# A TensorE-bound mixture-of-experts kernel: all SBUF buffers laid out in another order and at rounder addresses

## What is computed

```python
x = x + 0.5 * ffn(layernorm(x)); x = x + attn(layernorm(x)); x = x + 0.5 * ffn(layernorm(x))

def ffn(x):                                   # E = 64 experts, D = 128, F = 64, TOP_K = 8
    shared = silu(x @ Ws_up) @ Ws_down
    aff = x @ centroids.T
    idx = top_k(aff + expert_biases, 8)
    w = sigmoid(aff[idx]);  w = w / sum(w)    # cw: w at the 8 chosen experts, 0 at the others
    h = silu(einsum('td,edf->etf', x, W_up))
    y = einsum('etf,efd->etd', h, W_down)
    return shared + einsum('etd,te->td', y, cw)

def attn(u):
    xf = [u[0], u[1:] @ WB.T];  xb = [u[1:] @ WBf.T, u[-1]]
    gamma = sigmoid(xf @ w1.T + xb @ w2.T + b)
    return gamma * (xf + xb) + (1 - gamma) * u
```

## Time and profile before

| | before |
|---|---|
| median of three runs | 808.54 us |
| the profiled execution's own time | 808.82 us |
| its span (first to last instruction) | 806.9 us |
| TensorE, matmuls | 796.3 us busy (99%) |
| TensorE, weight loads (beside the matmuls) | 648.4 us (80%) |
| VectorE | 659.6 us (82%) |
| ScalarE | 627.3 us (78%) |
| GpSimd | 424.3 us (53%) |
| DMA | 11.44 MB, half of it (5.87 MB) in the first 40 us |

### The profile page before, as it was taken

One profiled execution on the slowest core, in us unless ns is written; L12 is line 12 of the kernel. 1 busy time (PEld: TensorE's weight loads), 2 busy tenths in 40 slices (PEclk: granted clock), 3 DMA queues, 4 the chain that ended last, 5 costly groups with the idle time before them and its releaser, 6 DMA issues.

```text
span 806.9 us, 12441 instructions
## 1 busy us (share of the span) xinstructions
PE 796.3 (99%) x3671; PEld 648.4 (80%) x3671; DVE 659.6 (82%) x1426; ACT 627.3 (78%) x1207; POOL 424.3 (53%) x378
## 2 busy tenths in 40 slices
PE   7999999999999999999999999999999999999998
PEld 5787878888888888888888888888888888888786
DVE  6887989779797788977879779797898788787875
ACT  5987777778877778868787678787788787786885
POOL 3885546454555554545545455464554545454453
PEclk9999999999999999999999999999999999999999
DMA  7100000000000000000000000000000000000000
GB/s 258 33 1 13 14 1 1 0 20 8 14 1 0 26 0 13 0 0 26 0 13 0 0 26 0 13 0 0 26 0 0 0 2 27 0 1 1 14 0 14
DMA packets 15901, 11.44 MB, mean 14 GB/s; under 512 B 1664, under 2 KB 14848, under 8 KB 15872
## 3 DMA queue, kind: packets, MB, share of 16 engines
q1 hardware_dynamic: 15872, 11.08, 4.4%
HBM read 8.98 MB, written 2.10 MB: 14 GB/s over the span
## 4 chain that ended last, share of the span: by engine, by line
PE 92%; DVE 3%; ACT 2%; POOL 2%; DMA 1%; SPq 0%; issue 0%; DVEq 0%
PE y_ps L772 14%; PE y_ps L774 14%; PE up L773 14%; PE up L772 14%; PE up L774 14%; PE y_ps L773 14%; PE side L781 3%; PE side L791 2%; PE side L813 1%; PE side L812 1%; POOL g_lo L362 1%; ACT g_hi L481 1%; ACT up L447 1%; DMA wu_raw<-in_w_up 1%; DVE gated L635 0%; DVE g_lo L644 0%
## 5 line engine op out<-in xcount | busy, mean ns | idle before, releaser
L362 POOL TENSOR_TENSOR g_lo<-gated,g_hi 128x512 fp32r<-128x512 f32 x256 | 333.6, 1303 | 339.9 <-ACT g_hi L481 339.1
L447 ACT ACTIVATE up<-up 128x512 f32<-128x512 f32 x513 | 300.2, 585 | 87.4 <-PE up L774 85.4
L635 DVE TENSOR_TENSOR gated<-up,cw 128x512 f32<-128x512 f32 x256 | 175.3, 685 | 85.0 <-ACT up L447 80.2
L772 PE MATMUL y_ps<-g_hi,wd_hi 128*128 128x512 f32 x512 | 207.5, 405 | 1.0 <-POOL g_lo L362 0.9
L772 PE MATMUL up<-x_hi,wu_hi 128*128 128x512 f32 x512 | 202.4, 395 | 0.8 <-POOL wu_lo L369 0.7
L773 PE MATMUL up<-x_lo,wu_hi 128*128 128x512 f32 x512 | 202.5, 396 | 0.0
L774 PE MATMUL y_ps<-g_hi,wd_lo 128*128 128x512 f32 x512 | 202.5, 396 | 0.0
L774 PE MATMUL up<-x_hi,wu_lo 128*128 128x512 f32 x512 | 201.8, 394 | 0.0
L773 PE MATMUL y_ps<-g_lo,wd_hi 128*128 128x512 f32 x512 | 201.5, 393 | 0.0
L635 DVE TENSOR_TENSOR up<-up,cw 128x512 f32<-128x512 f32 x256 | 176.5, 689 | 23.8 <-ACT up L447 18.7
L481 ACT CAST g_hi<-up 128x512 fp32r<-128x512 f32 x256 | 151.1, 590 | 45.5 <-DVE up L635 42.4
(11 more groups left out here) (114 smaller groups left out, 504.3 us busy)
## 6 DMA issues: line engine op xcount, KB each, us to landing
x_in<-in_x SPq DMA_DIRECT2D x8, 256.0 KB, 2.8
wu_raw<-in_w_up SPq DMA_DIRECT2D x4, 512.0 KB, 6.2
wd_raw<-in_w_down SPq DMA_DIRECT2D x4, 512.0 KB, 7.0
x_res<-in_x SPq DMA_DIRECT2D x8, 256.0 KB, 2.7
out<-out_sb SPq DMA_DIRECT2D x7, 256.0 KB, 2.2
out<-out_sb SPq DMA_DIRECT2D x2, 128.0 KB, 1.8
ident<-in_ident SPq DMA_DIRECT2D x1, 64.0 KB, 2.4
sm_raw<-in_ws_up SPq DMA_DIRECT2D x2, 32.0 KB, 2.3
```

What stands on the lines that cost most here:

```text
L362: nc.gpsimd.tensor_tensor(g_lo[:, i, :], gated[:, t // 2 % ORING, :], g_hi[:, i, :].bitcast(fp32), ALU.subtract).then_inc(lo_done[1], 1)
L447: nc.scalar.activation(up[i][:, :], up[i][:, :], ACT.Silu).then_inc(silu_done, 1)
L635: nc.vector.tensor_tensor(gated[:, t // 2 % ORING, :] if t % 2 else up[i][:, :], up[i][:, :], cw[ph.q][:, :], ALU.mult).then_inc(gate_done, 1)
L772: nc.tensor.matmul(o, a[0], b[0], start=start, stop=False)
```

## The change

The helper gets an argument for alignment, and the buffers are declared in another order: first the split weights, then the raw weights, `x_hi`, `x_lo`, `g_hi`, `g_lo`, then the other buffers of 2048 bytes or a multiple of it, all at multiples of 2048 bytes; then the smaller operands of TensorE at multiples of 512 bytes; then the rest as before. The instructions are the same ones in the same order on all five engines, with the same shapes, waits and semaphores; only the line numbers (three lower) and the addresses differ.

```diff
-        def sb(name, shape, dt=fp32):
-            return ctx.enter_context(nc.sbuf_tensor(name, shape, dt))
+        def sb(name, shape, dt=fp32, align=32):
+            return ctx.enter_context(nc.sbuf_tensor(name, shape, dt, align_bytes=align))
...
-        wu_raw, wd_raw = sb("wu_raw", [P, NJ, P]), sb("wd_raw", [P, NJ, P])
-        wu_hi, wu_lo = sb("wu_hi", [P, NJ, P], fp32r), sb("wu_lo", [P, NJ, P], fp32r)
-        wd_hi, wd_lo = sb("wd_hi", [P, NJ, P], fp32r), sb("wd_lo", [P, NJ, P], fp32r)
+        ROW = 512 * 4
+        wu_hi, wu_lo = sb("wu_hi", [P, NJ, P], fp32r, ROW), sb("wu_lo", [P, NJ, P], fp32r, ROW)
+        wd_hi, wd_lo = sb("wd_hi", [P, NJ, P], fp32r, ROW), sb("wd_lo", [P, NJ, P], fp32r, ROW)
+        wu_raw, wd_raw = sb("wu_raw", [P, NJ, P], fp32, ROW), sb("wd_raw", [P, NJ, P], fp32, ROW)
+
+        x_hi = [sb(f"x_hi{q}", [P, T], fp32r, ROW) for q in range(2)]
+        x_lo = [sb(f"x_lo{q}", [P, T], fp32r, ROW) for q in range(2)]
+        g_hi, g_lo = sb("g_hi", [P, GRING, T], fp32r, ROW), sb("g_lo", [P, GRING, T], fp32r, ROW)
+        x_raw = sb("x_raw", [P, T], fp32, ROW)
+        cw = [sb(f"cw{q}", [P, T], fp32, ROW) for q in range(2)]
+        gated = sb("gated", [P, ORING, T], fp32, ROW)
...
+        sm_hi, sm_lo = sb("sm_hi", [P, A1], fp32r, P * 4), sb("sm_lo", [P, A1], fp32r, P * 4)
+        su_both, su_high = sb("su_both", [P, P], fp32r, P * 4), sb("su_high", [P, P], fp32r, P * 4)
+        ident = sb("ident", [P, P], fp32, P * 4)
...
+        sm_raw = sb("sm_raw", [P, SW], fp32, P * 4)
+        u_mid = sb("u_mid", [P, T + 2], fp32, P * 4)
...
-        w_sel, w_dup = sb("w_sel", [P, NB, E + 1]), sb("w_dup", [P, NB, E, R])
+        w_sel, w_dup = sb("w_sel", [P, NB, E + 1]), sb("w_dup", [P, NB, E, R], fp32, P * 4)
```

More of the change, by code:

```diff
@@ L136, in build @@
     with ctx:
-        def sb(name, shape, dt=fp32):
-            return ctx.enter_context(nc.sbuf_tensor(name, shape, dt))
+        def sb(name, shape, dt=fp32, align=32):
+            return ctx.enter_context(nc.sbuf_tensor(name, shape, dt, align_bytes=align))
         def sem(name):
             return ctx.enter_context(nc.semaphore(name))
-        wu_raw, wd_raw = sb("wu_raw", [P, NJ, P]), sb("wd_raw", [P, NJ, P])
-        wu_hi, wu_lo = sb("wu_hi", [P, NJ, P], fp32r), sb("wu_lo", [P, NJ, P], fp32r)
-        wd_hi, wd_lo = sb("wd_hi", [P, NJ, P], fp32r), sb("wd_lo", [P, NJ, P], fp32r)
+        ROW = 512 * 4
[8 more added lines that the diff above has]
+        gated = sb("gated", [P, ORING, T], fp32, ROW)
+        sh_low = sb("sh_low", [F, T], fp32, ROW)
+        x_in, x_res = sb("x_in", [P, NB, D], fp32, ROW), sb("x_res", [P, NB, D], fp32, ROW)
+        x1, x2, x2_kept = (sb(n, [P, NB, D], fp32, ROW) for n in ("x1", "x2", "x2_kept"))
+        out_sb = sb("out_sb", [P, NB, D], fp32, ROW)
+        normed = [sb(f"normed{k}", [P, NB, D], fp32, ROW) for k in range(3)]
+        xu = sb("xu", [P, NB, D], fp32, ROW)
+        y_sb = sb("y_sb", [P, T], fp32, ROW)
         SU, SD = 0, P
@@ L152, in build @@
         SW = I2 + AW
[L153 to L159, removed]
+        sm_hi, sm_lo = sb("sm_hi", [P, A1], fp32r, P * 4), sb("sm_lo", [P, A1], fp32r, P * 4)
+        su_both, su_high = sb("su_both", [P, P], fp32r, P * 4), sb("su_high", [P, P], fp32r, P * 4)
+        ident = sb("ident", [P, P], fp32, P * 4)
+        wb_sb, wbf_sb = sb("wb_sb", [P, P], fp32, P * 4), sb("wbf_sb", [P, P], fp32, P * 4)
+        e0, e1 = sb("e0", [P, P], fp32, P * 4), sb("e1", [P, P], fp32, P * 4)
+        zeros_r = sb("zeros_r", [P, P], fp32r, P * 4)
+        sm_raw = sb("sm_raw", [P, SW], fp32, P * 4)
+        u_mid = sb("u_mid", [P, T + 2], fp32, P * 4)
         ce_raw = sb("ce_raw", [P, E])
-        wb_sb, wbf_sb = sb("wb_sb", [P, P]), sb("wbf_sb", [P, P])
-        ident = sb("ident", [P, P])
         bias_b = sb("bias_b", [P, E])
@@ L165, in build @@
         neg_half = sb("neg_half", [P, NB])
[L168 to L182, removed]
         stats = [sb(f"stats{k}", [P, NB, 6]) for k in range(3)]
@@ L187, in build @@
         th, gamma = sb("th", [P, NB]), sb("gamma", [P, NB])
-        u_mid = sb("u_mid", [P, T + 2])
-        e0, e1 = sb("e0", [P, P]), sb("e1", [P, P])
-        zeros_r = sb("zeros_r", [P, P], fp32r)
         sig, biased, taken = sb("sig", [P, NB, E]), sb("biased", [P, NB, E]), sb("taken", [P, NB, E])
         top = sb("top", [P, NB, TOPK])
-        w_sel, w_dup = sb("w_sel", [P, NB, E + 1]), sb("w_dup", [P, NB, E, R])
+        w_sel, w_dup = sb("w_sel", [P, NB, E + 1]), sb("w_dup", [P, NB, E, R], fp32, P * 4)
         w_sum, w_inv = sb("w_sum", [P, NB]), sb("w_inv", [P, NB])
```

## The result

The changed kernel takes 794.26 us, the median of six runs (794.14 to 794.77), against 808.50 us before (six runs, 808.38 to 808.57). The ratio is 0.9825, with a 95% interval of 0.9815 to 0.9835: 14.2 us or 1.75% faster. The forecast was no change, 808.5 us, with a range from 802.2 to 811.7; the time lies outside it.

The account below looks back on a forecast made before the run. The prediction took TensorE's matmul stream to bound the kernel, 3155 large matmuls at a pitch of 232.8 ns. Its terms, each taken at 0, summed to no change: 808.5 us, range 802.2 to 811.7 us.

Parts of the forecast that it names:

- The first step: Streams of the large matmuls no longer cross a multiple of 2048 bytes: taken at 0, at most 6.3 us less, far off 61.5.
- Rival 1: Crossing a 2048-byte multiple costs something in single-pass matmuls: 805.3 to 802.2 us if small, 747 us if large; chance 15%.
- Its sign: In the changed kernel's list by time, a large-matmul pitch of 231 ns or less would speak for Rival 1.
- The second step: Weight tiles no longer start 128 bytes past a multiple of 512: taken at 0, -2 to +2 ns a record, off the path.
- The indicator: Weight-load records of 188 ns again, and L812 and L813 at 275 and 274, would show The second step right.
- The third step: TensorE's weight and stream reads now both begin at remainder 0: taken at 0, from 2 ns less to 3 ns more.
- The witness: L768 in the first phase, weights and stream from the same address: mean 394 ns against 396 and 397, so no cost.
- The fourth step: Other engines on moved buffers, and the weights' first transfer: taken at 0, with 0.3 us either way for that transfer.
- A rhythm that may shift: Large matmuls' two pitches, 232.4 and 233.3 ns: the whole stream in one would take 1.6 us more or 1.3 us less.

## Why the prediction was wrong

- What bounds the kernel, and through what a layout could act, held: TensorE's pitch, nothing else, at the same clock.
- The first step, streams across a multiple of 2048: taken at 0, and it is 0 (808.53 us). Rival 1 named the right engine and sign and offered 802.2 to 805.3 us or 747 us, but its mechanism is refuted. Its sign, a pitch of 231 ns or less, came in all the same, since it is the sign of any gain in pitch.
- The second step, the weights' own start: taken at 0, and it is 0 (794.73 us with weights at 128). The indicator that I gave for it came in (records of 188, 274 and 274 ns, where I had named 188, 275 and 274), and said nothing of the pitch.
- The third step failed: "how the two reads of TensorE stand to each other". It was taken at 0 and is the whole change, 14.2 us, 4.5 ns a matmul. I asked only whether starting alike could cost something. It was the start before, 128 bytes apart by 256, that cost. The witness, three L768, has stream and weights starting together in the kernel before already, but three matmuls behind others at a difference of 128 don't settle, which takes about ten: their starts are 228 and 235 ns apart there and 227 and 227 in the changed kernel. In the run with the streams alone 128 bytes off they read the very addresses of the changed kernel and have 228 and 235 again, so what counts for them is what ran before. A mean record of 394 ns against 396 compared unsettled matmuls with dear ones. The bound drawn from it, 2 ns less to 3 ns more, was too narrow for that reason: 4.5 ns were due, and its lower end of 2 ns is 6.3 us, no further than the 802.2 us that the range had from the first step.
- The fourth step held: ScalarE and GpSimd are as fast as before. The first transfer took 4.42 us where the earlier trace rows have 4.92, and the first load of the experts' weights into TensorE came at 11.4 us where it was 11.9. I had allowed 0.3 us there. That half microsecond is not a share of the gain that comes from the pitch: with the streams alone moved it took 4.38 us, with that load at 11.4 us, in a kernel of 808.53 us.

```profile
4.92 4.42 DMA wu_raw<-in_w_up
```

- "A rhythm that may shift" saw that the same instructions have two pitches and took that for noise. It was a sign that the pitch hangs on how the reads follow each other: both are patterns of reads that start 128 bytes apart.

## What to carry to other kernels

When TensorE is busy all the time and the pitch of a 512-column fp32r matmul with 128 weight columns is some 233 ns, look at where stream and weights start: with all of them at one remainder by 256 bytes it was 226.7 ns, and one line of padding did it. Change that for all operands in a series together, since matching only pair by pair was slower than not at all (810.29 us). Expect less at other widths: at 384 columns a difference of 128 cost 2.5 ns, at 256 columns it was the cheaper one by 1.2. Read costs of a stream from the distance between starts over dozens of matmuls, and expect ten or so matmuls behind each interruption to run unsettled; a mean over three says nothing.

## What was not expected of the hardware

- TensorE's two reads interact. 512 columns at 2.4 GHz and one column a cycle are 213.3 ns (from 256 to 512 columns the pitch rose by 106.7 ns, which is that rate). The pitch was 226.7 ns at differences that are multiples of 256 bytes, 228.9 at 64, and 231.6 to 236.6 at all others tried. With 384 columns differences of 32 and 64 cost nothing.
- At difference 0, 256, 384 and 512 columns took 120.0, 173.4 and 226.7 ns: 13.3 ns over their columns each time. At difference 0 too, 448, 480 and 496 columns had 16.0 to 16.7 ns over theirs, and 512 columns with 8 to 96 weight columns 16.6 to 18.4. No series reached less than 13.3 ns over its columns, save 256 columns at difference 128, with 12.1.
- One set of remainders has more than one steady pitch: 232.4 and 233.3 ns in the kernel before.
- What stays open: what it is in the memory or in TensorE that makes the cost, which of the two reads pays it, what picks one steady pitch or another, and what the remaining 13.3 ns are. That the two reads meet in some unit of 256 bytes fits the multiples, but was not shown, and the reverse order at 256 columns speaks against so simple a picture.
